# First layer: the rescaling of all exponentials moved to GpSimd, and the split of queries and keys one step earlier

## The reference

```python
xn = _layernorm(x, axis=-1)
Q = (x @ Wq.T).reshape(b, n, H, R)          # H = 8 heads, R = 64
K = (x @ Wk.T).reshape(b, n, H, R)
V = (x @ Wv.T).reshape(b, n, H, d)
attn = jnp.einsum('bnhr,bmhr->bhnm', Q, K)
attn = jax.nn.softmax(attn, axis=-1)
out = jnp.einsum('bhnm,bmhd->bnd', attn, V)  # summed over the heads
x = x + attention(xn) + experts(xn)          # 8 experts, at most 80 tokens each, the best one per token
```

## Time and profile before

| what | value |
|---|---|
| time, median of three runs | 1526.85 us (1526.55 to 1529.49) |
| the profiled execution's own time | 1529.65 us |
| its span in the trace | 1527.9 us |
| first layer, first score maximum to the last AV matmul | 39.1 to about 423.8 us |
| busy over the whole span | PE 81%, DVE 84%, ACT 76%, POOL 52% |
| granted TensorE clock, mean of the span | 0.96 |

### The profile page before, as it was taken

One profiled execution on the slowest core, in us unless ns is written; L12 is line 12 of the kernel. 1 busy time (PEld: TensorE's weight loads), 2 busy tenths in 40 slices (PEclk: granted clock), 3 DMA queues, 4 the chain that ended last, 5 costly groups with the idle time before them and its releaser, 6 DMA issues.

```text
span 1527.9 us, 25209 instructions
## 1 busy us (share of the span) xinstructions
PE 1243.1 (81%) x6185; PEld 574.7 (38%) x6185; DVE 1288.3 (84%) x3505; ACT 1158.6 (76%) x1324; POOL 788.8 (52%) x1166
## 2 busy tenths in 40 slices
PE   2798687878763788888888888888888888888886
PEld 2466455555541223333233332333323333233333
DVE  5785687878865898999989999899998999989987
ACT  1565576777724888888888888888888888888860
POOL 2702100000000477777777777777777777777730
PEclk7799899999977899999999999999999999999998
DMA  5002100000000000000000000000000000000001
GB/s 179 13 1 37 12 1 0 0 0 0 0 1 18 14 18 18 18 28 24 17 17 17 28 24 17 17 17 28 24 17 17 17 28 24 17 17 17 27 24 31
DMA packets 38780, 31.58 MB, mean 21 GB/s; under 512 B 6150, under 2 KB 35609, under 8 KB 38738
## 3 DMA queue, kind: packets, MB, share of 16 engines
q1 hardware_dynamic: 37714, 29.76, 6.6%
q0 software_dynamic: 1024, 1.35, 0.8%
HBM read 29.10 MB, written 2.75 MB: 21 GB/s over the span
## 4 chain that ended last, share of the span: by engine, by line
PE 21%; DVE 19%; issue 14%; ACT 13%; DVEq 2%; ACTq 1%
DVE arena L1024 11%; ACT arena L1161 8%; PE ps L1304 7%; PE ps L1317 5%; ACT arena L1149 4%; DVE arena L1010 3%; PE ps L1353 3%; PE ps L1361 2%; PE ps L1381 2%; DVE z L1050 2%; DVE nmax L1016 1%; PE ps L1325 1%; DVEq L1067 1%; DVE x L1067 1%; DVEq L1023 1%
## 5 line engine op out<-in xcount | busy, mean ns | idle before, releaser
L1024 DVE SCALAR_TENSOR_TENSOR arena<-arena,ps 128x512 f32<-128x512 f32 x1024 | 665.7, 680 | 93.8 <-PE ps L1317 93.4
L1161 ACT ACTIVATE arena<-arena,eps 128x4096 f32<-128x4096 f32 x128 | 474.1, 3708 | 24.7 <-POOL arena L1284 24.2
L1278 POOL TENSOR_SCALAR arena<-kT,negq 128x512 f32<-128x512 f32 x480 | 330.9, 700 | 227.5 <-DVE arena L1024 218.9
L1317 PE MATMUL ps<-spread,sel 128*128 128x512 f16 x1024 | 357.6, 386 | 102.1 <-DVE arena L1024 95.9
L1284 POOL TENSOR_SCALAR arena<-arena,q 128x512 f32<-128x512 f32 x480 | 351.3, 741 | 22.4
L1304 PE MATMUL ps<-arena,phi_cols 128*32 128x512 f32 x2048 | 273.9, 609 | 53.9 <-ACT arena L1161 53.9
L1317 PEld LDWEIGHTS ps<-spread,sel 128*128 128x128 f16 x1024 | 94.4, 97 | 499.7 <-DVE arena L1024 400.6
L1149 ACT ACTIVATE arena<-kT,q 128x512 f32 (+1 forms) x330 | 217.3, 713 | 2.9
L489 ACT ACTIVATE kT<-ps,region 128x512 f32<-128x512 f32 x128 | 88.2, 689 | 105.8 <-DVE region L559 95.7
L1270 POOL TENSOR_SCALAR negq<-q 128x256 f32<-128x256 f32 x4 | 3.5, 868 | 299.8 <-POOLq L762 299.8
L1010 DVE TENSOR_SCALAR arena<-kT,q 128x512 f32 (+1 forms) x214 | 145.1, 701 | 0.3 <-PEq L762 0.3
(11 more groups left out here) (196 smaller groups left out, 1842.1 us busy)
## 6 DMA issues: line engine op xcount, KB each, us to landing
wge<-in_e_wg SPq DMA_DIRECT2D x32, 256.0 KB, 2.7
w1e<-in_e_w SPq DMA_DIRECT2D x32, 128.0 KB, 2.1
w2e<-in_e_w SPq DMA_DIRECT2D x32, 128.0 KB, 2.1
w3e<-in_e_w SPq DMA_DIRECT2D x32, 128.0 KB, 2.1
region<-in_w SPq DMA_DIRECT2D x1, 2048.0 KB
out<-x SPq DMA_DIRECT2D x4, 256.0 KB, 2.8
region<-in_wqk SPq DMA_DIRECT2D x1, 512.0 KB, 4.5
region<-in_wv SPq DMA_DIRECT2D x1, 512.0 KB, 5.2
```

The costliest lines, as they stand in the source:

```text
L1024: dve.scalar_tensor_tensor(feat[:, j, k, :], feat[:, j, k, :], 1.0, psB[:, k % BANKS, :], ALU.mult, ALU.mult, accum_out=sums[:, j, gg, c:c ...
L1161: act.activation(grp, grp, ACT.Sqrt, bias=eps[:]).then_inc(e_ready, 2)
L1278: pool.tensor_scalar(feat[:, j, QUADS * gg + c, :], kT[:, b * N:(b + 1) * N], HUGE, negq[:, b % 2, at - b * N // 2:at - b * N // 2 + 1], A ...
L1317: pe.matmul(psB[:, k % BANKS, :], sel[:, gg, c, :], spread[:, j, :], start=True, stop=True).then_inc(bc_done, 1)
```

## The change

ScalarE and VectorE no longer scale exponentials; GpSimd scales those of all 128 steps, each as soon as its reciprocal is there. The scatters stand between these: three before the first, one behind each of the next 13. The constants of the second layer are cut into 13 parts, one behind the rescale of steps 16 to 28 of row 0, and the gathers stand behind the rescales of steps 2 to 17 of row 1. The split of a next head's queries and keys stands in steps 0 (projection), 1 (high parts) and 2 (low parts) of a head instead of 1, 2 and 3. `prepare_constants` gets the number of the part to do.

```diff
-        ON_ACT = (2,)
-        QK_AT, QK_HI, QK_LO = 1, 2, 3
+        QK_AT, QK_HI, QK_LO = 0, 1, 2
+        SCATTERS_FIRST, CONSTANTS_AT, GATHERS_AT = 3, 16, 2
...
+            def rescale(n):
+                pool.wait_ge(rden_ready, n + 1)
+                pool.tensor_scalar(ex[:, n % 4, :], ex[:, n % 4, :], 1.0, rden[:, n % 4:n % 4 + 1],
+                                   ALU.mult, ALU.mult).then_inc(p_ready, 1)
+
+            pool.wait_ge(zeroed, 1)
+            for t in range(SCATTERS_FIRST):
+                scatter(t)
+            for b in range(B):
+                for s in range(STEPS):
+                    rescale(b * STEPS + s)
+                    if b == 0 and s + SCATTERS_FIRST < NT:
+                        scatter(s + SCATTERS_FIRST)
+                    if b == 0 and s >= CONSTANTS_AT:
+                        prepare_constants(pool, g, c2_made, c2_prep, s - CONSTANTS_AT)
+                    if b == 1 and 0 <= s - GATHERS_AT < NT:
+                        gather(s - GATHERS_AT)
             pool.wait_ge(gathered_in, 16 * NT)
...
-                    late = s - 1
-                    if late % TB in ON_ACT and runs(late, first, drain):
-                        act.wait_ge(rden_ready, b * STEPS + late + 1)
-                        act.activation(ex[:, late % 4, :], ex[:, late % 4, :], ACT.Copy,
-                                       scale=rden[:, late % 4:late % 4 + 1]).then_inc(act_p_ready, 1)
...
-                        if late % TB not in ON_ACT:
-                            dve.wait_ge(rden_ready, b * STEPS + late + 1)
-                            dve.tensor_scalar(ex[:, late % 4, :], ex[:, late % 4, :], rden[:, late % 4:late % 4 + 1], None,
-                                              ALU.mult).then_inc(p_ready, 1)
...
-                        if late % TB in ON_ACT:
-                            pe.wait_ge(act_p_ready, b * sum(by_act) + n)
-                        else:
-                            pe.wait_ge(p_ready, b * (STEPS - sum(by_act)) + late + 1 - n)
+                        pe.wait_ge(p_ready, b * STEPS + late + 1)
...
-def prepare_constants(pool, g, made, prep):
+def prepare_constants(pool, g, made, prep, part):
```

More of the change, by code:

```diff
@@ L401, in first_layer @@
         qk_done, qk_kept = sem("qk_done"), sem("qk_kept")
-        k_lo_filled, act_p_ready = sem("k_lo_filled"), sem("act_p_ready")
+        k_lo_filled = sem("k_lo_filled")
         q_hi_kept, k_hi_kept, v_hi_kept, lo_kept = (sem("q_hi_kept"), sem("k_hi_kept"), sem("v_hi_kept"),
@@ L444, in _, with scatter @@
             pool.memset(zero, 0.0).then_inc(zeroed, 1)
-            for t in range(NT):
+            def scatter(t):
                 pool.indirect_dma_start(
@@ L449, in _, with gather @@
                     g.xn[:, t, :], None, bounds_check=SLOTS - 1, oob_is_err=False).then_inc(g.scattered, 16)
[L450 to L453, removed]
+            def gather(t):
+                if t == 0:
+                    pool.wait_ge(eo_out, 16)
                 pool.indirect_dma_start(
@@ L668, in row @@
                     if runs(late, first, drain):
-                        by_act = [k % TB in ON_ACT for k in range(STEPS)]
-                        n = sum(by_act[:late % STEPS + 1]) - (sum(by_act) if late < 0 else 0)
-                        if late % TB in ON_ACT:
-                            pe.wait_ge(act_p_ready, b * sum(by_act) + n)
-                        else:
-                            pe.wait_ge(p_ready, b * (STEPS - sum(by_act)) + late + 1 - n)
+                        pe.wait_ge(p_ready, b * STEPS + late + 1)
                         if not first or late >= 2:
@@ L727, in _ @@
             row(B, drain=True)
-def prepare_constants(pool, g, made, prep):
[L732 to L741, removed]
-    v = g.sel[:].rearrange("p g c (h a) -> p g c h a", h=2)
-    for gg in range(GROUPS):
+def prepare_constants(pool, g, made, prep, part):
+    v = g.sel[:].rearrange("p g c (h a) -> p g c h a", h=2)
+    if part == 0:
+        pool.memset(g.sel[:], 0.0).then_inc(made, 1)
+    elif part == 1:
+        pool.memset(g.mask_c, 1.0).then_inc(made, 1)
+        pool.memset(g.phi_cols[:], 0.0)
+        pool.memset(g.weT[:, D:DV], 0.0)
+        pool.memset(g.V2[:, :, D:DV], 1.0)
+    elif part == 2:
+        pool.memset(g.sumsT[:], 0.0)
+        pool.memset(g.exT[:], 0.0)
+        pool.memset(g.eps[:], EPS_RHO)
+        pool.memset(g.rho, -math.sqrt(EPS_RHO))
+    elif part < 3 + GROUPS:
+        gg = part - 3
+        if gg == 0:
+            pool.wait_ge(made, 2)
         for half in range(2):
@@ L751, in prepare_constants @@
                 ins.then_inc(prep, 1)
[L752 to L756, removed]
+    elif part == 3 + GROUPS:
+        pool.affine_select(out=g.mask_c, in_=g.mask_c, compare_op=ALU.is_ge, fill=0.0, base=-16,
+                           pattern=[[-32, QUADS]], channel_multiplier=1).then_inc(made, 1)
+    elif part == 4 + GROUPS:
+        pool.wait_ge(made, 3)
+        pool.affine_select(out=g.mask_c, in_=g.mask_c, compare_op=ALU.is_ge, fill=0.0, base=31,
+                           pattern=[[32, QUADS]], channel_multiplier=-1).then_inc(made, 1)
 def second_route(nc, g, take):
```

## The result

The changed kernel took 1580.95 us (median of three, 1579.86 to 1583.45) against 1526.85: ratio 1.0352, 95% interval 1.0326 to 1.0378, or 54.1 us slower. The forecast was slower by 27 (1554, range 1537 to 1588). Sign and loop held. The size was off by a factor of two, and most of the missing half is what the first rival described, a TensorE clock that falls within the heads.

What follows compares the result with a forecast made beforehand. Bound by a loop of waits between engines, not one engine's work. Rows 1 to 3 26.1, row 0 7.7, drain 0.3, less 2.9 and 4.8 for stalls: +26.4 on 1526.85, rounded up to 1554 us; range 1537 to 1588.

Steps and rivals of the forecast that it cites:

- the first rival: Within heads, same loop, but TensorE's clock falls in every second of 28 heads: 34 us more, 1588; chance 0.19.
- The loop: Chain of waits between PE, ScalarE and VectorE that sets a head's time: 9.85 to 11.23 us, +1.38 a head.
- The clock: TensorE's clock within heads: taken as full in the sum, its fall left to a rival with chance 0.19.
- the rival's 2.4: Cost in us of each fall of TensorE's clock within a head, counted for every second of 28 heads.
- the product in step 3: Value product on PE in step 3 of heads 2 and 3: up to 0.86 us each, kept for the range.
- head 1: Second head of a row, held by the output of the row before, which the shift moves little: 0.
- the split's cost: Longer heads in row 0 from the earlier split: 6.9 + 0.8 = 7.7 us, bounds 0 to 14.
- the gain of the rescale: In row 0, VectorE no longer scales beside GpSimd's memset, so that stall leaves: -2.9 us.
- the stall: VectorE's scaling in row 0, 3.42 us beside a 3.54 us memset; said to leave, -2.9 us.
- The stand-still: In row 1 three engines stood still up to 9.67 us; spread gathers take away -9.7 to 0, middle -4.8.
- The rescale: Scaling moved from VectorE to GpSimd: hidden, at most 0.08 us a head to win; +0.3 us in the drain.

Runs made afterwards that it cites:

- e2: The kernel before with only the split moved to steps 0, 1 and 2, scaling still on VectorE and ScalarE: 1596.15 us, ratio 1.0525.
- e1: The changed kernel with the split back in steps 1, 2 and 3, the rescale still on GpSimd: 1510.43 us, ratio 0.9955.
- e7: The changed kernel with the split's low parts still in step 2 but behind the low part of the transposes: 1549.59 us, ratio 1.0134.
- e6_paced_gathers: The kernel before with each of the 16 gathers held back to a step of its own: 1517.17 us, ratio 1.0002.
- e8: The kernel before with its 16 gathers held back to a step each, run once more: 1516.6 us, ratio 1.0000.
- e9: The changed kernel with the split back in steps 1, 2 and 3, run once more: 1506.76 us, ratio 0.9929.
- e3: The changed kernel with 8 extra matmuls in PE's wait in step 3 of heads 4 to 7, rows 1 to 3: 1567.62 us, ratio 1.0344.

## Why the prediction was right, and where its size was off

**The loop: right.** Forecast 9.85 to 11.23 with the clock up; with the wait filled it measured 11.19, and the leg from maximum to transposes was 5.53 as forecast. e2 and e1 put the longer heads on the split alone, and e7 on the one wait that was named, PE's transposes of step 3 for the low part behind the split. The total still fell in the stated range only because that range reached up over the first rival; the forecast's own range ended at 1570, 11 us short.

**The clock: the term that was mis-sized.** The prediction walked the loop at full clock and gave a fall within the heads 0.19, "the wait is still shorter than the one that had the effect once in two". That reading overlooked a third wait of 3.09 in the same trace, at the start of row 1, which had slow matmuls behind it too, so it was twice in three:

```profile
146.23 0.79 PE L660 MATMUL ps<-k_hi,q_parts 128*128 128x512 f32 x1 [3.09 <-issue]
```

In the changed kernel the clock fell in each of the 18 heads with the wait of about 2.8, right behind it or within 1 us of matmuls. Priced per fall, the rival's 2.4 was near (1.3 to 2.3 in heads 4 to 6). Its count was too low, every second head in place of nearly all. In row 2: 109.31 less 88.86 is 20.45, against 8.7 forecast. What is missing is 11.8, or 1.5 for each of 8 heads. Heads 4 to 6 show 1.48, 1.28 and 2.27 above 11.23. Not all of it is the clock. In value heads the product in step 3, whose 0.86 the prediction left out of its sum and kept for the range, is on the loop with 0.8 at full clock (e7), and stands behind the wait, where it takes about twice that (1.91 by its row in e2). And head 1, priced at nothing, is 1.25 longer, with a fall of the clock in it.

**Row 0: the split's cost about right, the gain of the rescale too small.** From e1 to the changed kernel row 0 goes from 99.96 to 106.22, +6.3 (forecast +7.7). From the kernel before to e1 it goes from 108.48 to 99.96, -8.5 (forecast -2.9), but these traces are of different chips. On one chip it is -4.4 (e6_paced_gathers to e1) and -5.5 (e8 to e9), in line with scalings of 5.5 to 5.8 us beside the memset; the 3.42 on which the forecast went is the shortest of five. In the trace of before PE stood idle 5.57 us behind the stall and the clock was at half around it, while e1 has 0.88 in the like stretch:

```profile
50.40:64.00 13.60, 8.03 (x19) 4.12 (x17) 9.40 (x13) 4.66 (x11) 12.72 (x20) 0.50 0.09 26
...
53.00:67.00 14.00, 12.80 (x50) 8.12 (x49) 10.03 (x21) 9.49 (x21) 9.00 (x11) 0.88 0.02 5
```

How much of the stall's price is the clock was not separated.

**Row 1: the far end of the range.** The stand-still is gone wholly in the changed kernel (-9.7, forecast -4.8), and the row is 11.2 longer, which is 20.9 less 9.7. What makes it come and go on different chips was not settled.

**The rescale: right within the heads, too small at the row starts.** It was priced at nothing to 0.08 a head. Heads 4 to 6 of e1 give 0.04, and twice the price on GpSimd costs nothing. What the sum lacks is a gain at the row starts and ends: 3.1 us in row 2 (88.86 to 85.74 in e1), 3.4 to 3.7 on one chip (e8 to e9), with no stall there. What makes it was not examined. So the 20.45 of row 2 is a split that costs 23.6 (e1 to the changed kernel) less that gain. Moving the rescale is worth 6.5 to 10 us as a whole, on chips where the kernel before takes 1517. The split's new place spent that seven times over or more (73 us by the ends of the first layer in the two traces, 403.24 and 476.46).

Together: 26.4 forecast, 51.3 between the two profiled executions (54.1 by the medians); rows 1 to 3 bring 51.2 of it, in place of 21.3.

## What to carry to other kernels

In a software pipeline of several engines, moving one stage a step earlier does not make it earlier: ask which instructions of the busiest queue now lie between two passes of the slow hand-over, and add their time to the loop. Then ask how long that queue idles at one stretch, since a wait can be paid twice, once itself and once by the slower matmuls behind it. An engine relieved of work helps where it is in the loop (here not in heads 2 to 6, but at the row starts), and the table of busy shares does not say where that is.

## What the runs showed of the hardware that was not expected

PE idle times of 2.4 (e2) and 2.8 us were followed, at once or within 1 us, by matmuls at the lower of the two clocks (1.2 in place of 2.4 GHz; value matmuls 0.63 to 0.77 in place of 0.39 to 0.48), in all 18 heads of the changed kernel that had the one of about 2.8. Those of 1.97 to 1.99 in e7 were followed by full clock in all nine heads 4 to 6, but by the lower one in four of the six heads 2 and 3, and those of 3.09 before the change twice by the lower clock (at 146.23 and 245.56) and once by the full one. So the length of one wait did not settle it in these runs. Work for its own sake in the wait was worth more than it cost (e3). A VectorE scaling beside GpSimd's memset of 3.54 us took 3.42 us in one trace and 5.53 to 5.82 in four others. And the same kernel differed by 12 to 13 us between chips (1516.8 and 1529.8), with a stand-still of TensorE, VectorE and ScalarE for 7 to 10 us in both traces of the slower ones, and some 4 us more in row 0.
